# An attention step's probabilities: two short rows that TensorE transposed go by VectorE's 32x32 squares and DRAM like the other two

## The reference

```python
xn = layernorm(x)
qu, ku, vu, qc, kc, vc = heads(xn @ W_qkv.T)            # 8 heads of 64
term1 = where(future, 0, (qc*s) @ vu.T)                 # causal
look  = where(future, sigmoid((qu*s) @ ku.T), 0)
Su = term1 @ look.T
scores = (qc*s) @ kc.T - silu(Su);  scores[future] = -max
out = softmax(scores) @ vc                              # then @ W_out.T
x = x + out + (silu(xn @ Wg.T) * (xn @ Wu.T)) @ Wd.T    # hidden size 768
```

## Time and profile before

| | |
|---|---|
| Time, median of 3 runs | 1085.21 us (1083.92 to 1085.38) |
| Time of the profiled execution | 1081.44 us |
| Its span, first to last instruction | 1079.6 us |
| PE busy | 1039.0 us (96%) |
| DVE busy | 910.0 us (84%) |
| ACT busy | 752.2 us (70%) |
| POOL busy | 579.7 us (54%) |
| TensorE's granted clock | 1.0 of full speed in all slices |
| Transfers | 144.29 MB, mean 134 GB/s |

### The profile page before, as it was taken

The page is one execution under the profiler, slowest core; times in us unless marked ns, Lnnn a source line. Parts: engine busy times, 40 slices in busy tenths (PEclk is TensorE's granted clock), DMA queues, the critical chain, the costliest instruction groups (busy, mean ns, idle before and its releaser), DMA issues.

```text
span 1079.6 us, 21292 instructions
## 1 busy us (share of the span) xinstructions
PE 1039.0 (96%) x7472; PEld 923.8 (86%) x7472; DVE 910.0 (84%) x1801; ACT 752.2 (70%) x1423; POOL 579.7 (54%) x630
## 2 busy tenths in 40 slices
PE   6999999999999999999999999999999999999998
PEld 5878888888888888888888888888888878889997
DVE  5788899889998998899889988998888878676766
ACT  6667777877787778777877787778777775434333
POOL 5355565556555655565556555656555565422230
PEclk9999999999999999999999999999999999999999
DMA  5054645555555646465546554645354867546641
GB/s 195 1 108 93 144 122 118 127 119 147 108 137 106 160 102 140 102 162 107 130 104 161 111 127 110 163 93 120 79 132 86 230 177 249 175 168 200 221 153 60
DMA packets 362715, 144.29 MB, mean 134 GB/s; under 512 B 254832, under 2 KB 343664, under 8 KB 360560
## 3 DMA queue, kind: packets, MB, share of 16 engines
q1 hardware_dynamic: 362608, 142.91, 52.3%
HBM read 76.55 MB, written 66.32 MB: 132 GB/s over the span
## 4 chain that ended last, share of the span: by engine, by line
PE 71%; DVE 13%; ACT 9%; issue 4%; POOL 1%; DMA 0%; DVEq 0%; ACTq 0%; POOLq 0%
PE X L850 22%; PE X L765 11%; PE X L1001 7%; PE X L992 6%; PE X L902 6%; PE X L834 6%; PE X L804 5%; DVE PT_s L1545 4%; PE X L789 3%; PE X L818 3%; ACT prob L1191 3%; ACT T_s L1169 2%; PE X L884 2%; DVE prob L1502 2%; ACT L_s L1175 2%
## 5 line engine op out<-in xcount | busy, mean ns | idle before, releaser
L685 POOL TENSOR_SCALAR prob<-prob,inv 128x512 f32<-128x512 f32 (+3 forms) x256 | 301.7, 1194 | 6.1 <-DVE inv L1514 6.1
L850 PE MATMUL X<-L_s,T_s 128*128 128x128 f32 (+3 forms) x1920 | 276.0, 301 | 1.5 <-DVE L_s L1470 1.2
L850 PEld LDWEIGHTS X<-L_s,T_s 128*128 128x128 f32 x1920 | 265.4, 189 | 13.0 <-issue 2.3
L765 PE MATMUL X<-xT,W 128*128 128x512 f32 (+1 forms) x972 | 244.0, 398 | 0.0
L765 PEld LDWEIGHTS X<-xT,W 128*128 128x128 f32 x972 | 175.9, 191 | 40.1 <-issue 0.4
L1183 ACT ACTIVATE gate<-X 128x1024 f32<-128x1024 f32 (+1 forms) x96 | 84.8, 883 | 158.8 <-PE X L850 158.8
L659 POOL TENSOR_SCALAR_AFFINE_SELECT gate<-gate 128x256 f32<-128x256 f32 (+1 forms) x96 | 47.5, 494 | 204.7 <-DVE gate L1484 204.7
L675 POOL TENSOR_SCALAR_AFFINE_SELECT T_s<-T_s 128x512 fp32r<-128x512 f32 x128 | 104.6, 829 | 95.9 <-DVE T_s L1477 95.9
L1191 ACT ACTIVATE prob<-prob,least 128x512 f32<-128x512 f32 (+3 forms) x256 | 142.0, 591 | 1.5 <-DVE least L1502 1.5
L1477 DVE TENSOR_TENSOR T_s<-X,T_s 128x1024 fp32r<-128x1024 f32 (+1 forms) x96 | 100.1, 1043 | 37.5 <-ACT T_s L1169 37.5
L1484 DVE SCALAR_TENSOR_TENSOR gate<-gate,X 128x1024 f32<-128x1024 f32 (+1 forms) x96 | 97.1, 1038 | 37.7 <-ACT gate L1183 37.6
(11 more groups left out here) (111 smaller groups left out, 1867.3 us busy)
## 6 DMA issues: line engine op xcount, KB each, us to landing
PT_s<-prob_raw SPq DMA_DIRECT2D x210, 128.0 KB, 2.6
heads_out<-o_s SPq DMA_DIRECT2D x62, 256.0 KB, 3.5
prob_raw<-prob SPq DMA_DIRECT2D x120, 128.0 KB, 2.7
prob_raw<-prob SPq DMA_DIRECT2D x120, 96.0 KB, 2.8
xT_copy<-xT SPq DMA_DIRECT2D x8, 1024.0 KB, 7.0
w_split<-w_parts SPq DMA_DIRECT2D x22, 256.0 KB, 2.6
W<-w_split SPq DMA_DIRECT2D x12, 384.0 KB, 5.7
xT<-xT_copy SPq DMA_DIRECT2D x4, 1024.0 KB, 6.1
```

The source lines that it names most:

```text
L685: last = pool.tensor_scalar(v, v, inv[:, h, w - 1:w], None, ALU.mult)
L765: last = pe.matmul(out[:, tokens], sh.W[:, a, k, cols], xT[:, c, k, tokens], start=(n == 0), stop=(n == 3 * KD - 1))
L850: last = pe.matmul(both[:, h, at:at + (J + 1) * P], T_s[:, h, a, to:to + P], L_s[:, h, c, WIDE[J + 1]:WIDE[J + 1] + (J + 1) * P], start=(J ...
```

## The change

Rows 0 and 1 take the way of rows 3 and 2: a third `row_in_squares` of 768 columns on DVE, four more transfers out and three more back on SP. PE's `turn_heads` and the operations that emptied its banks are gone. `high_rows` and `low_rows` are now one operation of 1280 columns for each head; `attend` waits for each head's own low part, and the first head's stands ahead of the last `minus_scores`. On DVE, the projections' low parts and the three rows' squares are put in a new order, and the pieces of the next sequence's preparation go behind the first `silu_of` (but `ln.scale`, which goes ahead of it).

```diff
-         ("Su", 0, (2, 3)), ("PH", 0, (0, 1)), ("PT", 0, (0, 1)), ("PT", 1, (4,)), ("Su", 1, (6, 7)),
+         ("Su", 0, (2, 3)), ("PT", 0, (0, 1)), ("PT", 1, (4,)), ("Su", 1, (6, 7)),
...
SP step:
-                    for I in (3, 2):
+                    for I in (3, 2, 1):
                         spread_row(g - 1, I)
                     if back2:
                         sp.wait_ge(o_filled, 2 * g - 2)
-                    for I in (3, 2):
+                    for I in (3, 2, 1):
                         gather_row(g - 1, I)
...
gather_row:
-                for K in range(I + 1):
+                for i in (I, 0) if I == 1 else (I,):
+                    for K in range(i + 1):
...
PE attend, step:
-                        pe.wait_ge(PT_low, turned(g - 2, h))
-                        pe.wait_ge(rows_low, 2 * (g - 2) + 2)
+                        pe.wait_ge(rows_low, 2 * (g - 2) + h + 1)
...
-                if back1 and g - 1 < SQUARED:
-                    turn_heads(part, b, g)
...
ACT high_rows:
-                for I in (3, 2):
-                    act.wait_ge(row_loaded[I], (g + 1) * (I + 1) * 16)
-                act.activation(three_pairs(HIGH).bitcast(F32R), three_pairs(LOW), ACT.Copy).then_inc(rows_high, 1)
-                act.activation(PT_blocks[:, :, HIGH, 7, :].bitcast(F32R), PT_blocks[:, :, LOW, 7, :], ACT.Copy) \
-                   .then_inc(rows_high, 1)
+                for I in (3, 2, 1):
+                    act.wait_ge(row_loaded[I], (g + 1) * (I + 1 if I > 1 else 3) * 16)
+                for h in range(2):
+                    act.activation(PT_s[:, h, HIGH, :], PT_plain[:, h, LOW, :], ACT.Copy).then_inc(rows_high, 1)
...
DVE low_rows, step:
+            def low_rows(g, h):
+                dve.wait_ge(rows_high, 2 * g + h + 1)
+                dve.tensor_tensor(PT_s[:, h, LOW, :], PT_plain[:, h, LOW, :], PT_plain[:, h, HIGH, :], ALU.subtract) \
                    .then_inc(rows_low, 1)
...
                     minus_scores(g - 1, 1)
+                if back2 and g - 2 < SQUARED:
+                    low_rows(g - 2, 0)
                 if back1:
                     minus_scores(g - 1, 2)
                 if back2 and g - 2 < SQUARED:
-                    low_rows(g - 2)
+                    low_rows(g - 2, 1)
...
                     low_proj(g + 1, VU, par)
+                if ahead:
+                    low_proj(g + 1, QC, par)
                 if back1 and g - 1 < SQUARED:
                     row_in_squares(g - 1, 2)
-                if q == 1 and part != LAST:
-                    ln.scale(dve, b + 1)
-                if ahead:
-                    low_proj(g + 1, QC, par)
-                if q == 1 and part != LAST:
-                    turn_squares(b)
...
-                if q == 0 and part != LAST:
-                    ln.take_stats(dve, b + 1)
...
+                if back1 and g - 1 < SQUARED:
+                    row_in_squares(g - 1, 1)
+                if q == 1 and part != LAST:
+                    ln.scale(dve, b + 1)
...
                 silu_of(g, 0)
+                if q == 0 and part != LAST:
+                    ln.take_stats(dve, b + 1)
                 if q == 2 and part != LAST:
                     low_xT(b)
-                if back1 and g - 1 < SQUARED:
-                    low_heads(g - 1)
+                if q == 1 and part != LAST:
+                    turn_squares(b)
                 silu_of(g, 1)
```

More of the change, by code:

```diff
@@ L318, in layer @@
         prob_ready = sem("prob_ready")
-        row_in_squares_done = {I: sem(f"row{I}_in_squares") for I in (3, 2)}
-        row_spread = {I: sem(f"row{I}_spread") for I in (3, 2)}
-        row_loaded = {I: sem(f"row{I}_loaded") for I in (3, 2)}
+        row_in_squares_done = {I: sem(f"row{I}_in_squares") for I in (3, 2, 1)}
+        row_spread = {I: sem(f"row{I}_spread") for I in (3, 2, 1)}
+        row_loaded = {I: sem(f"row{I}_loaded") for I in (3, 2, 1)}
         rows_high = sem("rows_high")
@@ L426, in turned @@
         def turned(g, n):
-            return g + 1 if g < SQUARED else SQUARED + (g - SQUARED) * 3 + n + 1
+            return (g - SQUARED) * 3 + n + 1
         def emptied(kind, n, g, b):
@@ L876, in turn_probs @@
                 last.then_inc(PT_filled, 1)
[L878 to L886, removed]
             def attend(part, b, q, g, both=None):
@@ L944, in step @@
                 sum_up(part, b, g, 0)
-                if back1 and g - 1 < SQUARED:
-                    turn_heads(part, b, g)
-                elif back1:
+                if back1 and g - 1 >= SQUARED:
                     turn_probs(part, b, g, 0)
@@ L1386, in step @@
                 gate_of(g, 0)
-                if back1 and g - 1 < SQUARED:
-                    high_heads(g - 1)
-                elif back1:
+                if back1 and g - 1 >= SQUARED:
                     high_PT(g - 1, 0)
@@ L1493, in minus_scores @@
                 if j == 0 and not (isinstance(g, int) and g == 0):
-                    wait_before(dve, PT_filled, turned(g - 1, 1 if g - 1 < SQUARED else 2))
-                    if g - 1 < SQUARED:
-                        wait_before(dve, row_spread[3], g * 4 * 16)
-                if j == 1 and 0 <= g - 1 < SQUARED:
-                    wait_before(dve, row_spread[2], g * 4 * 16)
+                    if g - 1 >= SQUARED:
+                        wait_before(dve, PT_filled, turned(g - 1, 2))
+                if 0 <= g - 1 < SQUARED:
+                    for I in ((3,), (2, 1), (1,))[j]:
+                        wait_before(dve, row_spread[I], g * 4 * 16)
                 for h in range(2):
@@ L1769, in step @@
                     take_has_low(g - FIRST_CHUNK)
+                silu_of(g, 0)
+                if back1 and g - 1 >= SQUARED:
+                    low_PT(g - 1, 0)
+                    low_PT(g - 1, 1)
+                if q == 0 and part != LAST:
+                    ln.take_stats(dve, b + 1)
                 if q == 2 and part != LAST:
                     low_xT(b)
-                silu_of(g, 0)
-                if back1 and g - 1 < SQUARED:
-                    low_heads(g - 1)
-                elif back1:
-                    low_PT(g - 1, 0)
-                    low_PT(g - 1, 1)
+                if q == 1 and part != LAST:
+                    turn_squares(b)
                 silu_of(g, 1)
@@ L1804, in build @@
     xT_raw = [nc.dram_tensor(f"xT_raw{b}", [TT, 8, 32, P], F32).ap() for b in range(BATCH)]
-    prob_raw = {I: [nc.dram_tensor(f"prob_raw{I}_{g}", [2, 4 * I + 4, 32, P], F32).ap() for g in range(SQUARED)] for I in (3, 2)}
+    prob_raw = {I: [nc.dram_tensor(f"prob_raw{I}_{g}", [2 * (4 * I + 4 if I > 1 else 12), 32, P], F32).ap() for g in range(SQUARED)] for I in (3, 2, 1)}
     heads_out = nc.dram_tensor("heads_out", [2, BATCH * INNER, SEQ], F32).ap()
```

40 lines of the change are left out of this document (12 added, 28 removed).

## The result

The kernel after takes 1114.21 us (median of 4 runs, 1113.39 to 1115.54) where the kernel before takes 1084.57 us beside it (4 runs, 1083.34 to 1085.38). The ratio is 1.0275, with a 95% interval of 1.0258 to 1.0293: 2.75% slower. The forecast was 1093 us with a range of 1067 to 1108. The direction and the mechanism were those forecast; the time lies 6 us beyond the upper end. The span of the profiled execution is 1111.6 us in place of 1079.6, and that execution took 1113.46 us.

A forecast was written before the change was run, and what follows sets the result against it. PE bounded the kernel, with a hidden transfer loop of 22.2 us; the change makes it 26.8, with delays about 27.55. Four steps sum to 110.65 us against 109.46, +8 us overall: 1089.5 profiled, plus 3.8 gives 1093 us, range 1067 to 1108.

The forecast's parts named there:

- The transfers bind and the kernel is slower: Likeliest case: SP's added transfers out and back set the step; 1087 to 1104 us, chance 0.43.
- the sign posts: Expected trace: no L884, steps of 27.2 to 28 us, ACT idle up to 2 us before high_rows, PE waiting at attend.
- the loop: Chain ACT's rounding, DVE's squares, SP's transfers out and back, ACT again: 26.8 us without delays, 27.55 to 27.6 on average.
- the last landing: From the start of SP's last fetch issue until its data lands for ACT: 2.6 us.
- the delays: Extra time in SP's stretch of issues, scaled from 0.55 us by 22/15 issues: 0.8 us a step, bounds 0 and 1.1.
- ACT's rounding to the first spread: From ACT rounding a pair's rows to SP's first transfer out, DVE's low_rows and squares between: 12.3 us.
- The issues without delays: SP's undisturbed stretch of twelve issues out in 7.1 us and ten back in 5.1 us: 12.4 us.
- 1.79 and 1.5 us: DVE's two low_rows of 1280 columns: 1.79 us for head 0 beside POOL's norm, 1.5 for head 1.
- DVE's pace: Rival: transfers land in time and DVE sets steps; 1078 us, or 1068 with them wholly hidden; chance 0.33.
- The port: Rival: POOL's norm holds up DVE's first low_rows 1.0 us more; 1121 us, 1107 with half; chance 0.07.
- The wait at attend: PE's idle of 0.58 us before attend, 16.5 us in all, costs 0 to 0.1 us with head 0's low_rows earlier.
- The undisturbed stretch before: SP's stretch from first spread to last fetch in the kernel before, 15 issues: 8.6 us in half of the steps.

The follow-up runs named there:

- The idle transfers: Kernel before with seven transfers that nobody reads in each step from 2 to 29, between spreading and fetching: 1112.25 us, ratio 1.0267.
- the kernel without the third row: Kernel before plus low parts split by head and DVE's new order, PE still transposing rows 0 and 1 (turn_heads kept): 1076.42 us, ratio 0.9936.
- by head alone: Kernel before with only low_rows split by head, the first ahead of the last minus_scores; DVE's other order and transfers unchanged: 1094.16 us, ratio 1.0093.
- the kernel that beat both: Change with turn_heads kept, no third-row transfers; POOL norms rows 0 and 1 first, last group's reciprocal earlier, row 2's squares later: 1066.00 us, ratio 0.9840.

## Why the prediction was right or wrong

**The mechanism: right.** "The transfers bind and the kernel is slower", the likeliest case, is what happened, and the sign posts stand in the trace: no L884, ACT idle before `high_rows` behind DRAM, DVE before `low_rows`, PE at `attend`, twelve and ten issues on SP. The idle transfers show it from the other side. Three details were off. The steps with q = 1 are hidden like the others and no more regular; the longest wait is 3.7 us and not 2; and PE at `attend` waits for the last `minus_scores`, which empties its banks, where the prediction had only head 0's low part.

**The size: too small, and this is what failed.** The prediction had 27.55 us for the loop, and 28.43 were measured. Two terms of its sum were too small, the last landing (2.6 us where 3.06 were measured) and the delays (0.8 us where 1.10 were). By its own terms:

- *ACT's rounding to the first spread*: 12.3 foreseen, 12.32 measured. This was luck: two errors cancelled. `low_rows` was cheaper than 1.79 and 1.5 us: the mean of the 60 is 1.51, and start to start it is 1.41 for head 1 (534.42 to 535.83). But DVE then stood 0.5 to 0.6 us before the reciprocal for ACT's exponentials, a wait that I had not in the sum; ACT, with its two roundings in one place, had become late next.
- *The issues without delays*: 12.4 foreseen, and 12.46 to 12.48 measured in the three shortest stretches. Right. One of them, in which the instruction queue q8 moved nothing (a smaller one, q14, moved one packet):

```profile
400.80 7.22 SPq L563 DMA_DIRECT2D prob_raw<-prob  x12
408.12 5.14 SPq L572 DMA_DIRECT2D PT_s<-prob_raw  x10
```

- *The delays*: 0.8 us foreseen, 1.10 measured on average (13.56 less 12.46). The step "some 0.55 x 22/15 = 0.8", that delays grow with the number of issues, failed. The instruction queue moves as many packets after as before (60 against 61), but 25 of the 29 stretches after have one in them (13.70 us on average; 12.65 in the other four), and 11 of 29 before (9.76 against 8.53). For the stretch from 543.21 the DMA queues show:

```profile
q8 instruction: 1, 0.02, 0.6%
```

The packets do not come evenly over the step. In the kernel before, 17 of the 29 steps have one between 20.7 and 25.9 us behind ACT's rounding; there the stretch had ended at 20.7 on average (11.70 + 9.00), and after the change, with again 17 packets in that time, it ends at 25.9 (12.32 + 13.56). The trace of the kernel before could have told this. By the two pairs of means a caught packet goes with 1.05 to 1.2 us. That the packet is the cause of the delay is inferred from this company; no run takes the packets away. The upper bound of the prediction, 1.1 us, was the right value.

- *The last landing*: 2.6 us from the start of the last issue foreseen, 3.06 measured (0.51 of issue and 2.55 behind it). This was the worse of the two: +0.46 us in every step. 2.6 is the median landing of one transfer, and ACT waits for the latest of ten. It is no new effect: in the kernel before, the latest of the seven had landed 2.98 us after the start of the last issue (mean of 29), and 3.01 after the change. The prediction had that end as well ("27.3, with a landing counted from the end of the issue") and chose the other.

The sum: +0.30 for the delays, +0.46 for the landing, and about 0.1 in the other two terms and in rounding make the 0.88 by which 28.43 exceeds 27.55. The forecast's mean over the four kinds of step was 27.66 us (110.65 / 4), since two of them were foreseen longer than the loop. 29 times the 0.77 us missing are 22 us, which makes 1112 of the forecast 1089.5 for the profiled execution; it took 1113.5. Adding 3.8 us for the distance between execution and median was wrong in its turn: here it is 0.75. It goes with the clock: the profiled execution before had a granted clock of 1.000, and of the later executions of that kernel the five with 1.000 took 1081.35 to 1082.48 us, those with 0.997 or 0.998 took 1082.37 to 1084.73. The four executions after are all at 0.993 to 0.995. Seen from the kernel before, (28.43 - 27.28) x 29 = 33 us, against 32.0 in the span.

**The range** put the two ends of these terms into the bounds (26.2 to 27.3 without delays, 0 to 1.1 with), whose upper corner, 28.4 us, is what was measured. By the prediction's own sum a step of 28.4 us in all four kinds gives about 1115 us; but the likeliest case's own range ended at 1104 us and the whole at 1108, as if not both terms could be at their ends.

**DVE's pace: right, and hidden.** Without the transfers the kernel runs in 1063.76 us; the rival of DVE's pace was priced at 1068. So the change's work on the engines gains 1.8%, and its seven transfers cost more than that gain and 2.75% on top. The two do not add: +28 us for the transfers on the kernel before and -20 for the rest would be +8, but a step takes the longer of two periods, and the engines' gain vanishes under the loop.

**The port: false as a loss of DVE.** After the change DVE's two operations took 1.48 to 1.77 us, the mean being 1.51. In most steps, though, they come late and meet little of POOL's norm. The kernel without row 1's transfers is the better test: there head 0's `low_rows` falls on the norm in every step, and it took 1.49 or 1.50 us in 29 of 30, with 3.86 us for the norm's pair where the earlier trace rows have 3.11:

```profile
531.17 3.86 POOL L687 TENSOR_SCALAR prob<-prob,inv 128x512 f32<-128x512 f32 x2
...
532.11 1.49 DVE L1516 TENSOR_TENSOR PT_s<-PT_s 128x1280 fp32r<-128x1280 f32 x1 [0.17 <-ACT PT_s L1201]
```

So the 1.79 us of the sum were too much, and it was POOL that paid. After the change its mask of the tanh (L669) took 0.79 us in the step shown and up to 1.64 beside `low_rows`, where a free one takes 0.42; before, the same mask took 1.05 us beside `low_rows` in 28 steps. That costs nothing here, as POOL has idle time. The Trainium skill's page "SBUF — State Buffer", section "Who interferes with whom", has the later engine wait for the earlier. POOL's lengthened operations agree with it. The row of 1.49 us does not: this `low_rows` began while the norm's first operation was under way (531.17 to 532.74), and took no longer for it.

**The wait at attend: right on the edit, wrong by itself.** That the wait costs nothing once `low_rows(0)` is ahead was borne out by the kernel without the third row. That each edit could be costed alone was not: by head alone it moved the wait to `turn_heads` and doubled it for q = 1.

**Slips of reading**, none of which moves the result. DVE's free time in the four windows is 2.1 to 3.8 us and not from 1.1 on (27.07 - 25.00 in the earlier trace rows). The undisturbed stretch before is 8.46 us by the earlier trace rows (561.62 - 553.16) and not 8.6. And `low_rows` took 1.75 us in two steps, not one (735.36 and 869.89), both with POOL's second norm operation lengthened behind it.

## What to carry to other kernels

A hidden chain that closes on itself once a step has a period like an engine: add its issues, its longest landing (the latest of the group that is waited for, not the median of one) and the work that starts it, and compare that sum with the step before loading it further. A queue that is full for a larger part of the step also catches more of the disturbances in it. So delays read off a short stretch are not to be raised by the count of its issues: look in the trace for how many disturbances lie where the longer stretch will reach (here 11 stretches of 29 with a packet became 25). Before two operations change places on an engine, list everything that waits for the one that now comes later, the banks that it empties too. And a wait that is taken away by reordering one engine reappears at the next consumer unless that one's input comes sooner too; the kernel that beat both did just this, by making first what is wanted first.

## What the hardware showed beyond that

The granted clock of TensorE is 1.000 on average before and 0.994 after. PE stood 2.11 us before `attend` at 591.71, and the sixteen matmuls behind the wait took 4.01 us, where one step earlier, behind a wait of 0.67 us, they took 2.90:

```profile
562.76 2.90 PE L893 MATMUL X<-PT_s,v_s 128*128 128x512 f32 x16 [0.67 <-DVE least L1481]
```

```profile
591.71 4.01 PE L893 MATMUL X<-PT_s,v_s 128*128 128x512 f32 x16 [2.11 <-DVE least L1481]
```

The windows around it (the clock is the figure behind the five busy times) show the lower of the two levels, 1.2 GHz in place of 2.4:

```profile
593.00:594.00 1.00, 1.00 (x5) 0.86 (x4) 1.00 (x3) 1.00 (x4) 0.13 (x1) 0.53 1.14 435
594.00:595.00 1.00, 1.00 (x5) 0.90 (x5) 0.83 (x1) 1.00 (x6) 1.00 (x1) 0.50 0.99 406
```

There are four such stretches in this kernel ahead of its last microseconds, and each began within 1.4 us of PE's start behind an idle time, of 1.94, 2.72, 2.11 and 3.54 us; behind the other idle times at `attend`, of 1.71 us and less, there was none. The length alone does not decide it, though: in the kernel that has the low parts by head alone, PE stood 2.05 to 2.13 us before `turn_heads` in seven steps, and the clock fell behind three of them. After the change it costs nothing in the loop, since the transfers set the pace and PE waits again: the three loops with such a stretch take 28.13, 28.71 and 28.37 us, where the mean is 28.43. Where PE does set the pace it costs 1.6 us, as the two windows of that other kernel show (28.55 and 30.14 us).

Also new: fetches of the same size land 0.6 us later when two queues issue at once (3.3 against 2.7 us), so a second queue for a chain that waits for its last landing gives back part of what it saves.
